# The residual of the fifth norm by an accumulating transfer, and new orders on all engines

## What is computed

```
x = _layernorm(x + _L0_gnn_ref(x, L0_gnn_a, adj, adj))                # attention with a pair norm
x = _layernorm(x + _L1_gnn_ref(x, adj, Wp, bp, a_src, a_dst, ...))    # GAT, then GIN with an MLP
x = _layernorm(x + _L2_gnn_ref(x, adj, W, e, bias))                   # softmax over edge values
x = _layernorm(x + _L3_gnn_ref(x, adj, W, a_src, a_dst))              # GAT, elu
```

## Time and profile before

| | us |
|---|---|
| median of 3 runs | 1199.55 |
| lowest and highest | 1198.19, 1200.08 |
| the profiled execution, its own time | 1201.41 |
| its span, first to last instruction | 1199.5 |
| one turn in the steady part | 34.02 |

### The profile page before, as it was taken

The page is one execution under the profiler, slowest core; times in us unless marked ns, Lnnn a source line. Parts: engine busy times, 40 slices in busy tenths (PEclk is TensorE's granted clock), DMA queues, the critical chain, the costliest instruction groups (busy, mean ns, idle before and its releaser), DMA issues.

```text
span 1199.5 us, 29294 instructions
## 1 busy us (share of the span) xinstructions
PE 1115.1 (93%) x7721; PEld 913.9 (76%) x7752; DVE 1082.1 (90%) x4214; ACT 1012.0 (84%) x2581; POOL 405.5 (34%) x800
## 2 busy tenths in 40 slices
PE   4778999999999999999999999999999999999864
PEld 3456788888777778888777788887777788878653
DVE  6898999999999999999999999999999999997542
ACT  3456799999999999999999999999999999998654
POOL 3122334423334344323433344233343443233211
PEclk9699999999999999999999999999999999999876
DMA  3000011011011111010011110110111100100000
GB/s 84 27 19 28 27 37 36 20 33 35 17 35 35 35 35 33 20 35 26 26 35 35 35 35 17 35 35 18 35 35 35 35 27 25 36 27 11 19 9 18
DMA packets 59459, 35.95 MB, mean 30 GB/s; under 512 B 3872, under 2 KB 54816, under 8 KB 59424
## 3 DMA queue, kind: packets, MB, share of 16 engines
q1 hardware_dynamic: 59424, 35.54, 9.7%
HBM read 18.75 MB, written 8.39 MB: 23 GB/s over the span
## 4 chain that ended last, share of the span: by engine, by line
DVE 46%; issue 28%; POOL 12%; PE 8%; ACT 2%; DVEq 2%; POOLq 0%; DMA 0%; ACTq 0%; SPq 0%
DVE wB L1116 5%; DVE pTB L1147 5%; DVE vA L1226 4%; DVE wE L1116 3%; DVE vA L1245 3%; DVE wE L1134 3%; POOL rirA L450 3%; POOL lnr_E L438 2%; POOL lnr_B L438 2%; DVE lnst_B L1268 2%; DVE lnst_D L1088 2%; DVE lnst_C L1088 2%; DVE t2B L1301 2%; DVE lnst_Z L1088 1%; DVE y_D L1318 1%
## 5 line engine op out<-in xcount | busy, mean ns | idle before, releaser
L750 PE MATMUL ps<-hE,pTE 128*128 128x128 f32 x1024 | 133.7, 279 | 0.1
L432 POOL TENSOR_TENSOR lnve_Z<-lnmv_Z,consts 128x4 f32<-128x4 f32 x32 | 17.1, 534 | 330.8 <-DVE lnmv_Z L1096 330.8
L678 PE MATMUL ps<-xsA,pA 128*128 128x128 f32 x1024 | 124.3, 281 | 1.2 <-ACT xsA L1555 1.2
L750 PE MATMUL ps<-hB,pTB 128*128 128x128 f32 x1024 | 124.9, 275 | 0.0
L750 PEld LDWEIGHTS ps<-hE,pTE 128*128 128x128 f32 x1024 | 122.8, 193 | 2.3 <-issue 0.6
L810 PE MATMUL ps<-att_j,xD 128*128 128x512 f32 x256 | 124.3, 609 | 0.0
L767 PE MATMUL ps<-gin_j,hgat 128*128 128x512 f32 x256 | 121.7, 599 | 0.0
L678 PEld LDWEIGHTS ps<-xsA,pA 128*128 128x128 f32 x1024 | 119.1, 195 | 1.5 <-ACT xsA L1555 1.3
L750 PEld LDWEIGHTS ps<-hB,pTB 128*128 128x128 f32 x1024 | 119.4, 192 | 0.2 <-issue 0.2
L1116 DVE SCALAR_TENSOR_TENSOR wE<-ps,hE,y2E 128x512 f32<-128x512 f32 x128 | 90.0, 745 | 24.8 <-ACT y2E L1577 21.5
L1545 ACT ACTIVATE pA<-vA,nmA,rirA 128x512 f32<-128x512 f32 x128 | 104.6, 818 | 4.7 <-DVE vA L1245 4.7
(11 more groups left out here) (237 smaller groups left out, 3040.9 us busy)
## 6 DMA issues: line engine op xcount, KB each, us to landing
xA<-in_x_dram SPq DMA_DIRECT2D x32, 256.0 KB, 2.6
xrA<-in_x_dram SPq DMA_DIRECT2D x32, 256.0 KB, 2.7
xrB<-xB SPq DMA_DIRECT2D x32, 256.0 KB, 2.2
out_dram<-xout SPq DMA_DIRECT2D x32, 256.0 KB, 2.2
adj_i<-in_adj_dram SPq DMA_DIRECT2D x1, 1024.0 KB, 5.2
a<-in_L_gnn_a_dram SPq DMA_DIRECT2D x2, 64.0 KB, 5.6
w_sb<-in_L_gnn_W_dram SPq DMA_DIRECT2D x2, 64.0 KB, 4.5
l2w<-in_L_gnn_W_dram SPq DMA_DIRECT2D x2, 64.0 KB, 3.7
```

The lines of the kernel that those rows point to most:

```text
L678: last = mm(at("aggA")[:, i * P:(i + 1) * P], pA[:, j, i * P:(i + 1) * P], xsA[:, j], start=(j == 0), stop=(j == NT - 1))
L750: last = mm(at("agg" + n)[:, i * P:(i + 1) * P], att[n]["pT"][:, i, j], att[n]["h"][:, j, 0:P], start=(j == 0), stop=(j == NT - 1))
```

## The change

DVE's `y_E` is taken out. `y1_E` writes `min(euE, 1) + ruE` to the norm's input tile and leaves the -1 out, and POOL issues a transfer from `xE` that adds to that tile. `bn_E` and `norm_D` wait for the transfer's semaphore. One wait of `L_B0` and `L_E0` goes, for a transposition that the next wait implies. The banks' uses, the order of the setup's signals and the orders and delays in the `turn` of SP, POOL, PE, DVE and ACT are all new. The number of turns is the same.

```diff
+            def y_E(g):
+                pool.wait_ge(s["y1E"], 1)
+                pool.wait_ge(s["y1E"], g.now)
+                pool.dma_start(ln["E"]["y"][:], xE[:], accum_op=ALU.add).then_inc(s["yE_added"], 16)
...
             def turn(t):
-                t.run(rstd_A, 2)
+                t.once(no_edge_E, 4)
                 t.run(rstd_Z, 3)
-                t.once(numbers, 0)
-                t.once(no_edge_E, 4)
                 t.run(rstd_D, 4)
-                t.once(loops_E, 2)
+                t.once(triangles, 1)
+                t.run(y_E, 5)
                 t.run(rstd_C, 3)
                 t.run(rstd_B, 2)
+                t.once(loops_E, 1)
+                t.once(numbers, 0)
                 t.run(rstd_E, 5)
-                t.once(triangles, 1)
+                t.run(rstd_A, 1)
                 t.run(power_A, 0)
...
-                    dve.wait_ge(s["y_" + k] if src is None else s["z_in_psum"], g.now)
+                    if k == "E":
+                        dve.wait_ge(s["yE_added"], 16 * g.now)
+                    else:
+                        dve.wait_ge(s["y_" + k] if src is None else s["z_in_psum"], g.now)
...
-                        dve.wait_ge(s[f"t{n}_in_psum"], g.now)
...
-                v.scalar_tensor_tensor(y1E[:], euE[:], 1.0, ruE[:], ALU.min, ALU.add).then_inc(s["y1E"], 1)
-
-            def y_E(g):
-                dve.wait_ge(s["y1E"], g.now)
                 dve.wait_ge(s["applied_E"], g.last)
-                v.scalar_tensor_tensor(ln["E"]["y"][:], y1E[:], -1.0, xE[:], ALU.add, ALU.add).then_inc(s["y_E"], 1)
+                v.scalar_tensor_tensor(ln["E"]["y"][:], euE[:], 1.0, ruE[:], ALU.min, ALU.add).then_inc(s["y1E"], 1)
...
-                act.wait_ge(s["y_E"], g.last)
+                act.wait_ge(s["yE_added"], 16 * g.last)
```

More of the change, by code:

```diff
@@ L1354, in turn @@
-                t.run(join_A, 1)
-                t.once(edge_numbers, 0)
-                t.run(gain_B, 2)
-                t.once(past_table1, 1)
+                t.once(past_table2, 1)
+                t.run(bn_A, 1)
+                t.run(mean_A, 0)
+                t.once(outside0, 1)
+                t.run(join_A, 1)
+                t.run(centre_A, 0)
+                t.run(gain_B, 2)
+                t.once(outside1, 1)
+                t.run(square_A, 0)
+                t.run(offset_B, 2)
@@ L1358, in turn @@
+                t.once(row_minimum0, 1)
+                t.run(L_E0, 4)
+                t.once(edge_numbers, 0)
+                t.run(sumsq_A, 0)
+                t.once(self_loops, 2)
+                t.once(outside2, 1)
+                t.run(variance_A, 0)
+                t.run(L_E1, 4)
+                t.once(no_edge_B, 0)
+                t.once(bias_row1, 1)
+                t.once(row_minimum1, 1)
+                t.run(M_E0, 4)
                 t.run(shift_A, 0)
-                t.once(past_table2, 1)
+                t.once(row_minimum2, 1)
@@ L1371, in turn @@
[L1371 to L1375 removed]
+                t.once(outside3, 1)
+                t.once(mask_adj, 0)
+                t.once(normal_rows0, 1)
+                t.run(L_E2, 4)
                 t.run(M_E1, 4)
[L1377 removed]
                 t.run(L_E3, 4)
[L1379 to L1380 removed]
@@ L1418, in turn @@
+                t.once(clip_count2, 0)
+                t.run(mult_B1, 1)
+                t.run(lrelu_A3, 0)
+                t.run(y1_E, 4)
+                t.once(select_rows1, 0)
+                t.once(normal_rows1, 1)
+                t.once(clip_count3, 0)
+                t.run(mult_B2, 1)
+                t.run(q_C, 2)
                 t.once(split_high, 0)
-                t.run(q_C, 2)
-                t.once(row_minimum0, 1)
-                t.run(mult_B1, 1)
                 t.run(recip_A, 0)
-                t.run(mult_B2, 1)
+                t.once(edge_ranks, 0)
@@ L1424, in turn @@
+                t.once(split_rest0, 0)
+                t.run(mult_B3, 1)
+                t.once(match_edges0, 0)
                 t.run(y_C, 2)
-                t.run(mult_B3, 1)
+                t.run(zz_B, 1)
+                t.once(normal_rows2, 1)
+                t.once(bias_row0, 0)
+                t.once(split_middle, 0)
+                t.once(match_edges1, 0)
+                t.once(past_table0, 0)
                 t.run(bn_C, 2)
-                t.run(y1_E, 4)
-                t.once(outside2, 1)
@@ L1429, in turn @@
-                t.once(normal_rows0, 1)
                 t.run(join_C, 2)
-                t.once(clip_count1, 0)
-                t.run(y_E, 4)
                 t.run(bn_B, 1)
-                t.run(zz_B, 1)
-                t.once(row_ranges, 0)
-                t.once(self_loops, 1)
+                t.once(normal_rows3, 1)
                 t.run(bn_E, 4)
-                t.once(select_rows0, 0)
                 t.run(join_B, 1)
-                t.once(clip_count2, 0)
+                t.run(stats_B, 1)
@@ L1696, in turn @@
+                t.once(exp_rows3, 2)
+                t.run(copy_xTE, 4)
                 t.run(norm_C, 3)
-                t.once(copy_adj3, 0)
-                t.run(tanh_A, 1)
-                t.run(copy_xTE, 4)
-                t.run(norm_B, 2)
-                t.once(copy_no_edge, 1)
-                t.run(copy_h012E, 4)
-                t.once(copy_gin, 0)
-                t.run(copy_h3E, 4)
-                t.run(norm_E, 5)
-                t.run(y2_E, 4)
-                t.once(copy_sel0, 1)
@@ L1708, in turn @@
-                t.run(relu_B, 2)
+                t.run(tanh_A, 1)
+                t.run(copy_h012E, 4)
+                t.once(copy_sel1, 1)
+                t.once(exp_rows0, 1)
+                t.run(copy_h3E, 4)
+                t.run(norm_B, 2)
+                t.run(y2_E, 4)
+                t.once(copy_att0, 2)
+                t.once(copy_att1, 2)
+                t.run(norm_E, 5)
+                t.run(relu_B, 2)
+                t.once(copy_adj3, 0)
                 t.run(copy_xTD, 3)
-                t.once(exp_rows2, 2)
```

251 lines of the change are left out of this document (114 added, 137 removed), and 14 rows, old and new, of the table IN_BANK.

## The result

The changed kernel takes 1219.87 us (median of 4 runs, 1218.45 to 1221.36), the kernel before 1199.74 beside it: a ratio of 1.0166, 95% interval 1.0154 to 1.0178. It is slower, by 20 us or 1.7%. The profiled execution has a span of 1219.3 us, 19.8 more than before.

The account below looks back on a forecast made before the run. DVE, with PE and ACT close behind, was taken as the bound. Turns -8.6 us (0.32 over 27), start -2, end +2.5 sum to -8.1: forecast 1191 us, 8-in-10 range 1176 to 1217, own range 1186 to 1196, chance 0.37.

Parts of the forecast that it names:

- The removed slot: On DVE, taking out `y_E` frees one slot of 0.57 us per turn; DVE alone would give 33.45 us.
- rival 2: DVE alone sets the turn, D below 2.95: turn 33.45 or 33.3 us, time 1182 us; chance 0.23.
- The price D: Transfer latency from the end of `y1_E` to the semaphore: 2.2 + 1.0 = 3.2 us, upper end 6.7.
- Hidden until D = 2.95: At `norm_D`, the transfer costs nothing up to 4.6 - 1.67 = 2.95 us; at D = 3.2 it costs 0.25.
- the prediction's formula: Before `transpose_xE`, each microsecond of D beyond 2.95 is one of PE; idle about 0.25 us expected.
- The formula's ACT idle: ACT stands idle before `norm_D` for D - 2.7 us, released by the transfer.
- The loop from `gain_B` to `gain_B`: The longest loop, through DVE, PE and ACT: 33.5 us, 33.75 with the transfer's 0.25, rounded to 33.7.
- The DVE leg: From `gain_B` to the end of `mult_B3` on DVE: 25.0 us of the loop.
- the other leg: From `agg_B3` through `transpose_xE`, `copy_xTE`, `norm_C`, `tanh_A`, h copies and `norm_B`, with hand-overs: 8.5 us.
- Rival 1: The transfer lands late at `norm_D`: D = 3.9, turn 34.45, time 1212 us; chance 0.21.
- The start: Load of `a` issued before `adj`, setup parts spread anew: 2 us gained, between 0 and 5.
- The end: The last graph's `y_E`, 0.65 us before, becomes a transfer of 3.2 with nothing to hide behind: +2.5 us.

Follow-up runs that it names:

- the turn with the sum: Changed kernel's orders with the residual summed by `y_E` on DVE again and no transfer: 1208.82 us, turn 34.05.
- the spare copy: Changed kernel, but the accumulating transfer reads a spare copy of `xE` that SP makes by a plain transfer: 1190.03 us, ratio 0.9919.
- half: Changed kernel with only two of the four tiles (128 KB) in the accumulating transfer, the rest of the residual left out: 1202.14 us, turn 33.66.
- the run with the old orders: Kernel before with its own orders, `y_E` taken off DVE and put as a transfer on POOL behind `rstd_D`: 1334.56 us, ratio 1.1122.
- the old orders with the earlier `y1_E`: Kernel before's orders with the transfer and `relu_E`, `expm_E`, `y1_E` moved earlier: 1249.35 us reading `xE`, 1241.58 us reading a spare copy.
- the placement alone: Kernel before with only once-only steps moved, selection and counts ahead of `recip_A` on DVE and `agg_A0` on PE: 1205.20 us, ratio 1.0040.

## Why the prediction was wrong

- **The removed slot.** About right. DVE alone, with nothing of `norm_D`'s wait, takes 33.31 us a turn (predicted 33.45, or 33.3 in rival 2). In the same orders the turn with the sum and that with the spare copy are 0.70 apart, where the slot was taken as 0.57.
- **The price D.** This term was mis-sized. The landing was taken as 3.2 and is 3.3, so the 1.0 us added for a second pass of bytes came out; that the second pass is the reason is not shown. But D was defined from the end of `y1_E`, and no term was given to the way from there to POOL's instruction: 0.55 us. D is 3.85. The hand-over was left out in the one place where a whole turn hangs on it.
- **Hidden until D = 2.95.** Right in its number, in part by luck: the line meets the floor at 2.96. But PE, priced at 4.6 us from the end of `y1_E` to a free `transpose_xE`, took 4.86 (619.85 less 0.69 of idle time, less 614.30), and less 1.70 for `norm_D` that would give 3.16. PE's idle time by the prediction's formula would be 0.90 at D = 3.85; it was 0.69. The formula's ACT idle, D - 2.7, gives 1.15 and 0.55 for whole and half; 1.26 and 0.65 were measured. From 33.31, D - 2.95 more gives 34.21; 34.20 was measured.
- **The loop from `gain_B` to `gain_B`.** The DVE leg, 25.0, is 24.92 (`gain_B` at 591.23 to the end of `mult_B3` at 616.15). But the other leg doesn't close at `gain_B`: it closes at `y_A`, which waits for `tanh_A`. The walk passed `y_A`, and took `norm_C` and `tanh_A` as work ahead of `norm_B` only. The sum was still near, since `gain_B` stands 2.05 us behind `y_A` and `norm_B` takes 1.5: with D = 3.2 the measured line gives 33.55, against 33.7.
- **Rival 1** is what happened in the steady turn: D = 3.9, turn 34.45, mechanism and place (`norm_D`) right, break-even D = 3.47 where the line gives 3.67 (34.02 - 33.31 + 2.96).
- **The start.** This step failed altogether: -2 us, between 0 and -5, against +10.6 (-1.0 and +11.6). The first `dots_A0` came 1.0 us earlier in this trace, and 0.1 to 0.4 in the other kernels with these loads. "The setup parts are spread anew" was given no cost: the bound allowed only a gain. The new orders have `select_rows` and `clip_count` ahead of `recip_A` in DVE's turn 0, and `fetch_counts1` ahead of `agg_A0` on PE; walking turn 0 as the steady turn was walked would have shown the placement that costs 4.9 us. Where the other 6.7 come from stays open.
- **The end.** +2.5 predicted, +3.1 measured: the last `bn_E` starts 3.85 us after the end of `y1_E`, against 0.76 before (1191.22 to 1191.98). The difference is again mostly the hand-over. The +3.3 of the table is near by chance, since its stretch holds several more turns that gain and lose. The last `bn_E` waits for the whole transfer:

```profile
1211.38 0.87 DVE L1099 BATCH_NORM_STATS2 lnst_E<-y_E 128x6 f32<-128x128 f32 x4 [3.85 <-DMA y_E<-xE]
```

Against the forecast of -8.1 the sum is 28 us off: 12.6 from the start, 13.6 from turns 6 to 30 (25 x 0.32 = 8.0 hoped for, 5.6 lost), the rest from turns 4 and 5 and the end. Rival 1 with the measured start would have come to 1212 + 12.6 = 1225, 5 us above the 1219.87.

## What to carry to other kernels

A transfer in place of a sum holds its source for as long as its destination: ask first who writes the source next, and if that is near, read from a spare copy that a plain transfer makes while nothing waits (here 30 us of 1220). Measure such a latency from the end of the producer, with the hand-over to the issuing engine as a term, and beside the transfers that will run with it (3.85 us here, 4.6 where two others were issued with it). And where orders are changed, walk the first turn, with its once-only work, as carefully as the steady one: four turns of the start lost more here (11.6 us) than 27 steady turns were to gain (8.6).

## What the runs showed of the hardware

POOL's transfer instruction starts 0.55 us after the end of what it waited for, also where POOL had been idle for 3.79 us (`y1_E` ends at 700.37, the instruction starts at 700.93 in the run with the old orders); arithmetic on POOL started 0.1 us after its releaser (`lnve_C` in the earlier trace rows at 603.86; `join_C` started at 603.42 and took 0.36). The instruction itself takes 0.92 us.

The accumulating transfer from SBUF to SBUF landed 3.3, 2.7 and 2.4 us after its issue for 256, 128 and 64 KB, which is 2.1 us and 1.2 us per 256 KB. The Trainium skill (DMA: Bandwidth & Descriptors, Anatomy of one DMA — SWDGE) gives 2.0 us and the bytes at 436 GB/s for one transfer, without a figure for an accumulating one; an estimate by it is 2.6, 2.3 and 2.15 us. The trace agrees with the fixed part and not with the rest: the bytes cost twice as much, as if reading the destination counted as a pass of its own. No run here has a plain transfer on POOL's queue, so it isn't shown that the accumulation is the reason.

The same 256 KB landed 3.3 us after the issue where SP's `xrB` and `xA` were issued 1.9 and 2.7 us later, and 4.1 us where they were issued 0.1 and 1.7 to 1.9 us later (the old orders with the earlier `y1_E`). At the end of such a run, where no other transfer is under way and the engines are idle too, the time from `y1_E` to `bn_E` was that of 3.3 (3.84 us). The neighbours are thus the likely reason; no run moves them alone. The landing of `xrB` stayed at 2.2 to 2.3 us in all of them.

The same 32 matmuls of the first `agg_A` took 6.19, 4.24 and 3.79 us in three kernels. The stretches in the kernel before, the changed one, and the one with the placement alone (the figure before the DMA share is the granted clock, as a mean of its levels of 1.2 and 2.4 GHz):

```profile
29.77:35.96 6.19, 6.18 (x32) 5.99 (x32) 5.14 (x25) 0.00 (x0) 0.00 (x0) 0.60 0.15 45
```

```profile
39.06:43.30 4.24, 4.24 (x36) 4.23 (x35) 3.42 (x19) 0.00 (x0) 0.00 (x0) 0.88 0.01 3
```

```profile
36.87:40.66 3.79, 3.79 (x37) 3.79 (x34) 1.79 (x16) 0.00 (x0) 0.00 (x0) 1.00 0.00 0
```

In the kernel before, the granted clock was low for most of that stretch. In the third, PE had waited 5.03 us for the selection, and the low stretch lay ahead of `agg_A`: 0.52 from 33.00 to 36.87, while PE fetched and transposed the selection, then 1.00. This gave back 2.4 of the 7.1 us by which `agg_A` started later there.
